# Keys and queries of a fused attention and expert layer: transposed in 32 rows a head, with the repeated rows written by transfers

## The chip, the cores and the metric

The kernel runs on one core of a Trainium2 chip. The metric is the device time of one execution in microseconds (us). The engines named here are TensorE (PE in the rows; its weight loads are PEld), VectorE (DVE), ScalarE (ACT), GpSimd (POOL) and SyncE, whose queue (SPq) issues every transfer of this kernel and does nothing else.

## The reference, cut to what matters

The input x is (4, 1024, 256): 4 batches, 1024 positions, 256 channels. Two layers follow each other, all in float32:

- A gated recurrence: x is normalised, two projections are made, and `state = tanh(p_t + state)` runs over the 1024 positions, one after the other, for all batches and channels at once. The gated states are normalised and added to x.
- A block on the rows of each 256-position piece: causal attention within the piece with 16 heads of 16 channels, then four experts.

```
h = _rms(x, n1_w)
q = _rms(heads(wq), qn_w);  k = _rms(heads(wk), kn_w);  v = heads(wv)
scores = einsum('bhqd,bhkd->bhqk', q, k) * HD ** (-0.5)        # causal
x = x + ao                                                      # softmax(scores) @ v, then @ wo.T
moe = wts[:, 0:1]*o0 + wts[:, 1:2]*o1 + wts[:, 2:3]*o2 + wts[:, 3:4]*o3
```

All 1024 positions of a batch attend causally to the positions before them. The four experts are chains of two to four products with gelu or silu between them, weighted by a top-2 gate.

## The kernel before, in words

**Units.** The time axis is cut into 4 chunks of 256 positions. A unit `u` (0 to 15) is 256 rows of 4 batches by 4 chunks: `c, b = divmod(u, 4)`. In chunk 0 a unit holds one row tile of 128 positions of each of two batches, in the other chunks two row tiles (`s` = 0, 1) of one batch. A unit can begin when the recurrence has passed its last position. It goes through these steps: gate and normalise (`pgate`, `ptr`, `pln`, `pu`), the projections (`qk`, `vm`), keys and queries (`kh`, `kt`, `kc`, `kst`; `qq`, `qt`, `qc`), the row maxima of the scores (`ktm`, `mxm`, `mxr`), their transposition into a bound (`mtr`, `mta`, `mtd`), the scores and their exponentials (`kts`, `sc`, `ex`, `msk`), the product with the values (`vl`, `av`), the output projection, and the experts (`up`, `gel`, `dn`, `da`), whose weights are loaded again for each unit (`wr`, 27 loads a unit into 6 buffers `WB`).

**Recurrence.** Each of the 1023 steps is an addition on GpSimd (`sadd`, line 1702) and a tanh on ScalarE (`stanh`, line 928). ScalarE does the kernel's other activations between them.

**Order.** `arrange()` (line 249) lists every step with its engine, an assumed duration, a due time and the steps it follows; `Plan.run()` (line 112) plays this through and writes down one fixed order for each engine. The due times are tables in the source (`START`, `AT`). On the chip each engine runs its list in that order and waits on semaphores, so a late step holds back all that stand behind it on its engine. The assumed durations decide the order alone.

**Keys and queries before.** Products are float32 in a reduced form, so each key and query is split into a high part (hi) and a low part (lo), and the score is `khi*qhi + khi*qlo + klo*qhi`. A head takes 64 columns of `QKP`: for keys hi, hi, lo, for queries hi, lo, hi (16 each), then a column of ones and 15 of zeros. VectorE writes them (lines 1490 and 1492). TensorE transposes two heads at a time, 8 transposes a row tile (`kt`, `qt`, line 1126), into two banks of the accumulator memory (`P2`). ScalarE copies 1024 columns out (lines 979 and 987): queries straight into `QT`, where they stay, keys into `KTs`, from which 4 transfers a row tile (`kst`, line 850) store them into `ktd` in memory. From there they are loaded twice for each unit, once for the maxima (`ktm`, lines 861 and 863) and once for the scores (`kts`, lines 883 and 885), as 128 rows: 64 of an even head, 64 of an odd one. The products read 64 rows. Row 48 of the keys is one, and row 48 of the queries is one until `mtd` (line 872) overwrites it with the negated maximum.

The lines the change touches: 249 to 430 (the plan), 545 to 550 (how much a transfer adds to its semaphore), 636 to 641 and 709 (buffers), 845 to 886 (transfers), 974 to 988 (ScalarE's copies), 1120 to 1182 (transposes and products), 1471 to 1492 and 1505 to 1510 (VectorE), 1663 to 1693 (constants on GpSimd).

Of the kernel before, what the change touches and what calls it, by code (L numbers as in the profile page):

```python
# [5 lines left out]
F32 = mybir.dt.float32  # L6
F32R = mybir.dt.float32r
# [12 lines left out]
KR = 64  # L20
# [24 lines left out]
           "Vs": 1, "QKP": 1, "KTs": 1, "QT": 2, "KT": 3, "VL": 2, "PT": 3, "AVS": 2, "AO": 1, "TV": 1,  # L45
# [4 lines left out]
DRAIN = 0.25  # L50
# [4 lines left out]
WINDOW, LOW, HIGH, FRESH = 3.413, 0.38, 0.75, 80.0  # L55

STALL = {"wsh": 0.3, "wsp": 0.45, "gll": 0.45, "kh": 0.12, "pgate": 0.15, "qq": 0.06, "hsc": 0.05, "fin": 0.05, "pln": 0.03, "pu": 0.03}
# [3 lines left out]
AT = {"piece": (-65.1, 79.3, 93.0, 117.5),  # L61
      "post": (73.5, 53.5, -11.6, 4.0),
      "prep": (-32.9, -50.6, -75.5, -31.9),
      "value": (-168.0, 5.7, -122.1, -102.7),
      "key": (-92.9, -70.4, 23.2, -60.9),
      "query": (-70.1, -15.7, -105.7, -9.8),
      "max": (-55.3, -48.9, -46.0, -51.3),
      "maxima": (1.8, 4.8, 14.5, 33.1),
      "bound": (97.6, -38.5, 63.2, 74.1),
      "score": (20.8, 39.5, 20.4, 48.1),  # L70
      "scores": (18.6, 9.7, 15.8, 8.7),
      "av": (18.9, -22.6, 2.7, 0.5),
      "merge": (36.4, -20.4, -11.9, 0.7),
      "out": (-203.1, 8.4, -74.1, -92.8),
      "gate": (-58.6, -112.8, -61.9, -36.5),
      "l1": (38.7, 246.6, 204.8, 191.9),
      "e0up": (141.5, 167.2, 99.3, 296.6),
      "l2": (241.4, 262.9, 274.5, 274.1),
      "e0dn": (304.8, 265.3, 456.7, -58.1),
      "e1": (248.8, 254.1, 341.0, 226.9),  # L80
      "l3": (253.5, 307.5, 179.0, 266.6),
      "e3dn": (182.7, 315.9, 233.6, 257.0),
      "e1dn": (285.7, 322.0, 304.5, 354.3),
      "l4": (216.1, 314.5, 172.6, 308.5),
      "e3up": (250.0, 261.2, 290.1, 275.3),
      "e3out": (240.7, 251.3, 293.6, 381.5),
      "fin": (203.7, 196.0, 239.1, 437.5)}


class Plan:  # L90
# [21 lines left out]
    def run(self):  # L112
# [15 lines left out]
        while True:  # L128
# [4 lines left out]
            for e in ready:  # L133
# [115 lines left out]
def arrange():  # L249
# [51 lines left out]
    add("pool", ("consts",), 6.6, 1.0, ("ident",))  # L301
# [16 lines left out]
    for u in range(NU):  # L318
# [33 lines left out]
        for s in range(2):  # L352
            add("dve", ("kh", u, s), 2.33, d, ("qrs", u), ("cqk", 0), ("consts",), take={"QKP": (("kt", u, s),)})
# [4 lines left out]
            add("pe", ("qt", u, s), 0.645, d0 + at["query"], ("qq", u, s), mode="128", take={"P2": (("qc", u, s),), **({} if s else {"QT": (("sc", u, 3, nkb - 1),)})}, lat=DRAIN)  # L358
            add("act", ("qc", u, s), act(1024), d0 + at["query"], ("qt", u, s), *([("qc", u, 0)] if s else []))
# [5 lines left out]
        for j, (g, planes) in enumerate(jobs):  # L365
            dj = d + at["maxima"] * j / len(jobs)
            add("sp", ("ktm", u, j), 0.35, dj - 5, *keys, *([("ktm", *prior["ktm"])] if "ktm" in prior else []), lat=4.5, take={"KT": (("mxm", u, ends[j]),)})
            prior["ktm"] = (u, j)
            for i, (j_, s, pl, k0, w) in enumerate(tiles):
# [6 lines left out]
                add("pe", ("mxm", u, i), 0.02 + w / 2400 + (0.065 if diag else 0.0), dj, ("ktm", u, j), ("qc", u, 0), ("qc", u, 1), ("consts",),  # L376
# [11 lines left out]
        for g in range(4):  # L388
# [3 lines left out]
            for h in range((nkb + 3) // 4):  # L392
                lastkb = min(4 * h + 3, nkb - 1)
                add("sp", ("kts", u, g, h), 0.35, dg - 5, *keys, *([("kts", *prior["kts"])] if "kts" in prior else []), lat=4.5, take={"KT": (("sc", u, g, lastkb),)})
# [115 lines left out]
class Signals:  # L510
# [34 lines left out]
    def step(self, key):  # L545
        if key not in self.plan.transfers:
            return 1
        if key[0] in ("gl", "ktm", "kts", "vl") and key[1] < B:
            return 32
        return {"vst": 64, "kst": 64, "mtd": 32}.get(key[0], 16)  # L550
# [34 lines left out]
def build(nc, A, out):  # L585
    ctx = ExitStack()
    with ctx:
# [48 lines left out]
        QKP = sb("QKP", [128, HEADS, KR], F32R)  # L636
        MT = sb("MT", [16, L], F32R)
        KTs = sb("KTs", [128, 8, 128], F32R)
# [70 lines left out]
        ktd = dram("ktd", (B, 4, 128, 2, T))  # L709
# [29 lines left out]
        def _(eng):  # L739
# [7 lines left out]
            for key in plan.order["sp"]:  # L747
# [97 lines left out]
                elif kind == "kst":  # L845
# [893 lines left out]
```

## Time and profile before

| | |
|---|---|
| median of 3 runs | 1584.79 us (1576.91 to 1586.72) |
| the profiled execution's own time | 1589.69 us |
| span of its profile | 1588.0 us |
| mean granted TensorE clock | 0.933 |
| TensorE busy | 1403.0 us, 88% |
| VectorE busy | 1098.6 us, 69% |
| ScalarE busy | 952.3 us, 60% |
| GpSimd busy | 319.2 us, 20% |
| transfers | 278.54 MB, their queue at 56.6% of the 16 transfer engines |

Busy time is the time in which an engine has an instruction under way. The granted clock is a share of TensorE's full clock, 2.4 GHz; at 0.5 it runs at 1.2 GHz. The transfer engines move the data; the queue on SyncE only issues. A stretch A:B is in us from the start of the span.

### The profile page before, as it was taken

How to read it: one execution, taken by the hardware profiler on the slowest of the kernel's cores; microseconds unless marked ns; L12 is line 12 of the kernel's file. 1: busy time of each engine (PE TensorE's matmuls, PEld its weight loads, DVE VectorE, ACT ScalarE, POOL GpSimd, SP SyncE). 2: the span in 40 equal slices, each digit the busy share in tenths (PEclk: the TensorE clock that was granted, in tenths of full speed). 3: DMA queues.
4: the chain of work that ended last, by engine and by line, in shares of the span. 5: the costliest groups of instructions: out<-in, count | busy, mean ns of one | idle time of the engine just before them, and what ended most of it. 6: DMA issues, size and time to landing. Idle time of an engine off the chain costs nothing. (4 is left out here: it accounts for less than half of the span.)

```text
span 1588.0 us, 33694 instructions
## 1 busy us (share of the span) xinstructions
PE 1403.0 (88%) x12320; PEld 1108.8 (70%) x12320; DVE 1098.6 (69%) x2916; ACT 952.3 (60%) x2092; POOL 319.2 (20%) x1146
## 2 busy tenths in 40 slices
PE   6915679999979799998998999999999999999997
PEld 3404567889867568688885577876686667857697
DVE  7776577553886975858888569786788777773342
ACT  2535465675556777775555673538546676468941
POOL 3343333223333323232332110001000010000000
PEclk9956578999998999899998899999999999999999
DMA  5585336754675545546656455665656657556343
GB/s 170 147 285 151 112 103 195 217 152 142 181 227 184 184 138 169 184 125 201 204 177 191 150 161 168 223 193 153 205 178 207 202 170 216 180 189 202 123 144 112
DMA packets 244276, 278.54 MB, mean 175 GB/s; under 512 B 37136, under 2 KB 167696, under 8 KB 243856
## 3 DMA queue, kind: packets, MB, share of 16 engines
q1 hardware_dynamic: 244112, 276.39, 56.6%
q8 instruction: 99, 1.62, 0.4%
q14 instruction: 65, 0.53, 0.1%
HBM read 234.18 MB, written 43.45 MB: 175 GB/s over the span
## 5 line engine op out<-in xcount | busy, mean ns | idle before, releaser
L1702 POOL TENSOR_TENSOR AD<-PX 128x8 f32<-128x8 f32 x1023 | 250.4, 245 | 553.3 <-ACT PX L928 537.3
L928 ACT ACTIVATE PX<-AD 128x8 f32<-128x8 f32 x1023 | 219.3, 214 | 232.0 <-POOL AD L1702 229.8
L996 ACT ACTIVATE work<-PS 128x1024 f32<-128x1024 f32 (+1 forms) x312 | 288.7, 960 | 79.5 <-PE PS L1042 77.8
L1501 DVE TENSOR_REDUCE mx<-PS 128x2 f32<-128x1024 f32 (+3 forms) x256 | 256.7, 1020 | 81.0 <-PE PS L1042 79.9
L1042 PE MATMUL PS<-work,vlx 128*32 128x256 f32 (+2 forms) x2816 | 240.6, 381 | 18.3 <-ACT work L996 7.5
L1042 PE MATMUL PS<-EP,u_e_l 128*128 128x256 f32 x1024 | 199.4, 289 | 6.9 <-DVE EP L1367 4.5
L1709 POOL TENSOR_SCALAR_AFFINE_SELECT work<-work 128x512 f32<-128x512 f32 x96 | 63.8, 674 | 638.1 <-ACT work L996 637.9
L1042 PE MATMUL PS<-WB,work 128*128 128x192 f32 x1024 | 181.2, 330 | 3.6 <-ACT work L1021 1.3
L1021 ACT ACTIVATE work<-PS 128x512 f32<-128x512 f32 x176 | 104.2, 596 | 132.7 <-PE PS L1042 131.2
L1042 PE MATMUL PS<-EP,WB 128*128 128x256 f32 x640 | 182.3, 285 | 0.0
L1042 PE MATMUL PS<-KT,QT 64*128 64x512 f32 (+3 forms) x768 | 151.9, 434 | 27.8 <-DVE mx L1501 12.9
L1042 PEld LDWEIGHTS PS<-EP,u_e_l 128*128 128x128 f32 x1024 | 164.0, 192 | 14.8 <-issue 10.3
L1042 PEld LDWEIGHTS PS<-WB,work 128*128 128x128 f32 x1024 | 164.9, 190 | 10.0 <-issue 4.0
L1042 PE MATMUL PS<-XF,WB 128*128 128x256 f32 x576 | 163.5, 284 | 0.0
L1042 PEld LDWEIGHTS PS<-work,vlx 128*32 128x32 f32 (+1 forms) x2816 | 87.6, 115 | 103.3 <-issue 49.6
L1042 PE MATMUL PS<-QT,KT 64*128 64x256 f32 (+1 forms) x1344 | 142.7, 315 | 15.9 <-ACT work L996 7.1
L1042 PEld LDWEIGHTS PS<-QT,KT 64*128 64x128 f32 x1344 | 99.9, 193 | 66.3 <-issue 45.6
L1042 PEld LDWEIGHTS PS<-KT,QT 64*128 64x128 f32 x768 | 72.8, 197 | 75.6 <-issue 27.1
L1042 PEld LDWEIGHTS PS<-EP,WB 128*128 128x128 f32 x640 | 124.3, 194 | 0.0
L1501 DVE TENSOR_REDUCE mxb<-PS 128x2 f32<-128x256 f32 (+3 forms) x128 | 104.7, 818 | 14.4 <-PE PS L1042 14.1
L1042 PEld LDWEIGHTS PS<-XF,WB 128*128 128x128 f32 x576 | 111.2, 193 | 0.1
L1021 ACT ACT_TABLE_LOAD x58 | 74.4, 1283 | 53.3 <-PE PS L1042 52.6
(170 smaller groups left out, 2345.8 us busy)
## 6 DMA issues: line engine op xcount, KB each, us to landing
KT<-ktd SPq DMA_DIRECT2D x112, 512.0 KB, 4.8
WB<-wlo_e_l SPq DMA_DIRECT2D x160, 256.0 KB, 3.0
WB<-wlo_e_up SPq DMA_DIRECT2D x64, 256.0 KB, 3.0
ktd<-KTs SPq DMA_DIRECT2D x128, 128.0 KB, 2.2
WB<-wlo_e_w SPq DMA_DIRECT2D x64, 256.0 KB, 2.9
WB<-wdn_e_down SPq DMA_DIRECT2D x64, 192.0 KB, 2.7
KT<-ktd SPq DMA_DIRECT2D x48, 256.0 KB, 3.5
KT<-ktd SPq DMA_DIRECT2D x32, 384.0 KB, 4.1
```

The source lines that it names most:

```text
L928: eng.activation(cur, AD[n % 2], ACT.Tanh).then_inc(of(*key), 1)
L996: eng.activation(pt[:, :, :, q0:L], two("sc", *a).rearrange("p a (l q) -> p a l q", l=2)[:, :, :, q0:L], ACT.Exp).then_inc(of(*key), 1)
L1021: eng.activation(half_of(hidden(u, name), h), one("up", u, name, h), ACT.Gelu).then_inc(of(*key), 1)
L1042: return eng.matmul(o, l, r, start=start, stop=stop, skip_group_check=skip)
L1501: eng.tensor_reduce(o, two("mxm", *a)[:, :, 0:w], AX, ALU.max, negate=True).then_inc(of(*key), 1)
L1702: eng.tensor_tensor(AD[n % 2], PX[c % 2][:, :, :, t], PX[(n - 1) // L % 2][:, :, :, (n - 1) % L], ALU.add).then_inc(of(*key), 1)
L1709: eng.affine_select(out=p, in_=p, compare_op=ALU.is_ge, fill=0.0, base=0, pattern=[[0, 2], [0, 2], [1, 128]], channel_multiplier=-1).then_ ...
```

## The change

Each head gets 32 columns instead of 64: hi and lo, once each. There are two `QKP` buffers instead of one. Four heads make one transpose, so a row tile takes 4 transposes for keys and 4 for queries, into one bank (`P1`), and ScalarE copies 512 columns. The repeated rows are made by transfers:

- `kst` stores keys with 8 transfers a row tile instead of 4. Each of four heads' row blocks is written as 32 rows (hi, lo) and again 16 rows (hi). `ktd` now has 48 rows a head instead of 64.
- `qst` is new: the queries are copied to a staging buffer `QTs`, and 8 transfers a row tile move them within the core's memory into `QT` (16 rows hi, then 32 rows hi, lo). The maxima now wait for `qst` of the second row tile, where they waited for ScalarE's copy.
- Every key load of `ktm` and `kts` becomes two, one for each parity of the head, of 48 rows each.
- The maxima read 48 rows, the scores 49. The row of ones is no longer loaded; GpSimd fills the three `KT` buffers with ones at the start, in place of filling `QKP`. The addition of 1 in `mta` becomes a copy.
- The plan's assumed durations, its due times and the constants of its clock model are changed, so that every engine's order can differ from before.

```diff
-KR = 64
+KR = 32
-           "Vs": 1, "QKP": 1, "KTs": 1, "QT": 2, "KT": 3, ...
+           "Vs": 1, "QKP": 2, "KTs": 1, "QTs": 1, "QT": 2, "KT": 3, ...
[...]
[...]
+STREAM = {"ptr": 0.6, "qtr": 0.6, "xtr": 0.6, "aot": 0.6, "mgt": 0.6, "mtr": 0.6, "kt": 0.65, "qt": 0.65, "gm": 0.05, "htr": 0.5}
-STAY = {"pe": 18.5, "act": 7.0}
+STAY = {"pe": 31.5, "act": 6.8}
-START = (114.6, 163.8, 192.7, 269.5, 332.7, 421.8, 507.9, 597.9, 743.8, 801.4, 926.0, 996.4, 1096.7, 1187.3, 1295.6, 1383.6)
+START = (111.5, 169.3, 217.5, 285.7, 325.4, 421.8, 511.2, 594.7, 746.0, 799.4, 931.6, 974.7, 1099.6, 1177.1, 1290.4, 1382.0)
...
-                        streamed[w] += t - t0
+                        streamed[w] += (t - t0) * STREAM.get(k[0], 0.95)
...
-    add("pool", ("consts",), 6.6, 1.0, ("ident",))
+    add("pool", ("consts",), 9.0, 1.0, ("ident",))
...
-            add("dve", ("kh", u, s), 2.33, d, ..., take={"QKP": (("kt", u, s),)})
-            add("pe", ("kt", u, s), 0.645, d, ("kh", u, s), mode="128", take={"P2": (("kc", u, s),), "KTs": (("kst", u, s),)}, lat=DRAIN)
-            add("act", ("kc", u, s), act(1024), d, ("kt", u, s))
-            add("sp", ("kst", u, s), 1.0, d, ("kc", u, s), lat=2.5)
-            add("dve", ("qq", u, s), 0.93, d0 + at["query"], ("kh", u, s), ("kt", u, s), take={"QKP": (("qt", u, s),)})
-            ...
+            add("dve", ("kh", u, s), 2.06, d, ..., take={"QKP": (("kt", u, s),)})
+            add("pe", ("kt", u, s), 0.33, d, ("kh", u, s), mode="128", take={"P1": (("kc", u, s),), "KTs": (("kst", u, s),)}, lat=DRAIN)
+            add("act", ("kc", u, s), act(512), d, ("kt", u, s))
+            add("sp", ("kst", u, s), 2.0, d, ("kc", u, s), lat=2.5)
+            add("dve", ("qq", u, s), 0.66, d0 + at["query"], ("kh", u, s), take={"QKP": (("qt", u, s),)})
+            ...
+            add("sp", ("qst", u, s), 2.0, d0 + at["query"], ("qc", u, s), *([("qst", u, 0)] if s else []), lat=2.5,
+                take=None if s else {"QT": (("sc", u, 3, nkb - 1),)})
...
-            add("sp", ("ktm", u, j), 0.35, ...
+            add("sp", ("ktm", u, j), 0.5 if c else 1.0, ...
...
-        ktd = dram("ktd", (B, 4, 128, 2, T))
+        ktd = dram("ktd", (B, 4, 2, 48, 2, T))
...                                                    # kst
-                    for g in range(4):
-                        eng.dma_start(ktd[b, g, :, :, 128 * t:128 * t + 128],
-                                      plain(KTs[:, 2 * g:2 * g + 2, :])).then_inc(of(*key), 16)
+                    for pl in range(2):
+                        for par in range(2):
+                            h = 32 * (2 * pl + par)
+                            dst = ktd[b, :, par, :, pl, 128 * t:128 * t + 128].rearrange("g r t -> r g t")
+                            eng.dma_start(dst[0:32], plain(KTs[h:h + 32])).then_inc(of(*key), 16)
+                            eng.dma_start(dst[32:48], plain(KTs[h:h + 16])).then_inc(of(*key), 16)
+                elif kind == "qst":
+                    ...
+                    for pl in range(2):
+                        for par in range(2):
+                            h, dst = 32 * (2 * pl + par), qt[64 * par:64 * par + 48, :, pl, 128 * s:128 * s + 128]
+                            eng.dma_start(plain(dst[0:16]), plain(QTs[h:h + 16])).then_inc(of(*key), 16)
+                            eng.dma_start(plain(dst[16:48]), plain(QTs[h:h + 32])).then_inc(of(*key), 16)
...                                                    # kts, chunks 1 to 3; ktm alike
+                    sp.wait_ge(*done("consts"))
-                        eng.dma_start(plain(keys_of(kt, 2, n)),
-                                      ktd[u % B, g, :, :, 512 * h:512 * h + n]).then_inc(of(*key), 16)
+                        for par in range(2):
+                            eng.dma_start(plain(keys_of(kt, 2, n)[64 * par:64 * par + 48]),
+                                          ktd[u % B, g, par, :, :, 512 * h:512 * h + n]).then_inc(of(*key), 16)
...                                                    # kt and qt on TensorE
-                    for p in range(8):
-                        ins = eng.transpose(ps[:, p // 4, 128 * (p % 4):128 * (p % 4) + 128].bitcast(F32R),
-                                            QKP[:, 2 * p:2 * p + 2, :].rearrange("p h r -> p (h r)"), identr)
+                    for g in range(4):
+                        x = QKP[place[src, "QKP"]][:, 4 * g:4 * g + 4, :].rearrange("p h r -> p (h r)")
+                        ins = eng.transpose(one(*key)[:, 128 * g:128 * g + 128].bitcast(F32R), x, identr)
...                                                    # mxm, and sc with + 49
-                    pe.wait_ge(*latest([("qc", u, 0), ("qc", u, 1)]))
+                    pe.wait_ge(*done("qst", u, 1))
-                        rows = slice(64 * par, 64 * par + 64)
+                        rows = slice(64 * par, 64 * par + 48)
...                                                    # kh and qq on VectorE
-                    step(eng.tensor_copy(pair, x.unsqueeze(2).to_broadcast([128, 16, 2, 16])))
+                    step(eng.tensor_copy(hi, x))
-                    eng.tensor_tensor(QKP[:, :, low:low + 16], x, QKP[:, :, 0:16].bitcast(F32), ALU.subtract).then_inc(of(*key), 1)
+                    eng.tensor_tensor(lo, x, plain(hi), ALU.subtract).then_inc(of(*key), 1)
...                                                    # consts on GpSimd
-                    step(eng.memset(QKP.bitcast(F32), 0.0))
+                    for kt in KT:
+                        step(eng.memset(plain(kt), 1.0))
-                    step(eng.memset(QKP[:, :, 48:49].bitcast(F32), 1.0))
```

## Rows read from the trace of the kernel before

**Rows 1.** The page, its first part: busy us (share of the span) and instructions.

```profile
PE 1403.0 (88%) x12320; PEld 1108.8 (70%) x12320; DVE 1098.6 (69%) x2916; ACT 952.3 (60%) x2092; POOL 319.2 (20%) x1146
```

**Rows 2.** Busy time by stretch: stretch, us, each engine (instructions), granted clock, transfer share, GB/s.

```profile
100.00:200.00 100.00, 52.42 (x426) 42.11 (x426) 65.84 (x194) 48.12 (x175) 36.19 (x146) 0.59 0.51 154
200.00:300.00 100.00, 88.08 (x752) 76.09 (x744) 69.57 (x233) 63.36 (x191) 30.65 (x124) 0.85 0.55 164
...
1300.00:1400.00 100.00, 98.54 (x902) 78.38 (x901) 76.81 (x148) 58.88 (x74) 2.56 (x4) 1.00 0.64 192
```

**Rows 3.** Chain of waits from 860 us to the end, shares by engine and line.

```profile
by line: PE PS L1042 69.4%; ACT work L996 5.9%; issue 3.7%; DVE mx L1501 2.7%; PE PS L1045 2.1%; PE PS L1126 1.9%; DVE mxb L1501 1.7%; DMA KT<-ktd 1.4%; ACT L996 1.0%; ACT work L1021 0.8%; POOL work L1709 0.7%; ACT L1021 0.6%; DMA out<-UU 0
```

**Rows 4.** TensorE's order of work at 402 us: start, us, instructions, [idle before, releaser].

```profile
402.88 0.66 PE L1045 MATMUL PS<-ident,G 128*128 128x128 f32 x4 [1.03 <-DVE G L1413]
```

**Rows 5.** Who waited for whom: us in total, times, longest.

```profile
PE PS L1042 <- ACT work L996: 15.3, 32, 1.2
PE PS L1042 <- DMA KT<-ktd: 12.8, 7, 4.7
```

**Rows 6.** TensorE's order of work from 908 to 916 us.

```profile
908.66 0.74 PE L1042 MATMUL PS<-QT,KT 64*128 64x256 f32 x8
...
911.49 0.81 PE L1126 MATMUL PS<-identr,QKP 128*128 128x128 f32 x8
912.23 0.51 PE L1042 MATMUL PS<-QT,KT 64*128 64x256 f32 x4
...
914.10 1.70 PE L1042 MATMUL PS<-wqkv,hT 128*128 128x256 f32 x12
```

**Rows 7.** Line 1126 by stretch: stretch, us, PE busy, PEld busy, clock, transfer share, GB/s.

```profile
860.00:1588.00 728.00, 19.95 (x184) 17.02 (x184) 0.98 0.57 176
```

**Rows 8.** Groups by line and shape: count, busy us, mean ns, idle before.

```profile
L987 ACT ACTIVATE QT<-PS 128x1024 fp32r<-128x1024 f32 x32 | 32.8, 1024 | 13.6 <-PE PS L1126 13.5
L979 ACT ACTIVATE KTs<-PS 128x1024 fp32r<-128x1024 f32 x32 | 32.7, 1022 | 9.1 <-PE PS L1126 8.3
...
L1490 DVE CAST QKP<-QKB 128x512 fp32r<-128x512 f32 x64 | 29.2, 456 | 18.0 <-PE PS L1126 16.9
...
L972 ACT ACTIVATE Vs<-PS 128x512 f32<-128x512 f32 x16 | 9.6, 598 | 5.1 <-PE PS L1042 5.0
```

**Rows 9.** The page's groups, the score matmuls.

```profile
L1042 PE MATMUL PS<-QT,KT 64*128 64x256 f32 (+1 forms) x1344 | 142.7, 315 | 15.9 <-ACT work L996 7.1
```

**Rows 10.** Transfer issues by line: duration ns min/median/max, first and last start.

```profile
L850 SPq DMA_DIRECT2D ktd<-KTs x128: 513/620/1396, 139.1 to 1338.8; - x128
L861 SPq DMA_DIRECT2D KT<-ktd x32: 519/612/614, 149.8 to 305.4; - x32
L863 SPq DMA_DIRECT2D KT<-ktd x80: 319/374/638, 448.9 to 1427.3; - x80
L883 SPq DMA_DIRECT2D KT<-ktd x32: 517/612/1467, 163.3 to 336.5; - x32
L885 SPq DMA_DIRECT2D KT<-ktd x80: 517/524/951, 465.8 to 1486.0; - x80
L872 SPq DMA_DIRECT2D QT<-MT x32: 667/694/972, 176.6 to 1448.0; - x32
```

**Rows 11.** Transfers by form: issues, KB each, median us from issue to landing.

```profile
ktd<-KTs SPq DMA_DIRECT2D x128, 128.0 KB, 2.2
```

**Rows 12.** The first unit's stores and loads in the queue's order of time.

```profile
139.12 9.10 SPq L850 DMA_DIRECT2D ktd<-KTs  x8
149.82 3.84 SPq L861 DMA_DIRECT2D KT<-ktd  x6
```

**Rows 13.** The first products of maxima on TensorE.

```profile
153.09 0.33 PE L1042 MATMUL PS<-KT,QT 64*128 64x128 f32 x2 [2.38 <-DMA KT<-ktd]
```

**Rows 14.** What the queue waited for, us in total, times, longest.

```profile
SPq L794 <- PE PS L1042: 523.5, 246, 8.7
```

**Rows 15.** GpSimd's fill of QKP: duration ns, start.

```profile
L1672 POOL MEMSET QKP<- x1: 957/957/957, 2.9 to 2.9; 128x1024 f32 x1
```

More of the change, by code:

```diff
@@ new lines @@
+AT = {"piece": (-65.9, 153.7, 123.4, 201.4),
+      "post": (72.6, 37.5, 49.8, -40.7),
+      "prep": (-70.5, -85.7, -81.5, -49.3),
+      "value": (-130.5, -16.5, -90.8, -207.4),
+      "key": (-101.3, -93.8, 12.1, -50.7),
+      "query": (-72.5, -22.3, -74.4, 27.9),
+      "max": (-59.5, -56.5, -90.7, -58.8),
+      "maxima": (4.2, 6.9, 6.2, 38.7),
+      "bound": (92.1, -24.2, -6.7, 63.2),
+      "score": (12.1, 37.8, -26.2, 42.4),
+      "scores": (16.3, 10.1, 13.1, 9.8),
+      "av": (22.3, -28.9, 12.1, 9.6),
+      "merge": (38.1, -28.6, 7.6, -20.1),
+      "out": (-276.1, -58.2, -98.8, -100.5),
+      "gate": (-72.2, -98.2, 13.3, 92.2),
+      "l1": (78.2, 227.7, 186.3, 197.3),
+      "e0up": (117.8, 172.1, 107.2, 286.2),
+      "l2": (237.2, 278.9, 224.7, 314.6),
+      "e0dn": (310.5, 380.5, 428.4, -102.3),
+      "e1": (255.0, 249.6, 316.5, 264.8),
+      "l3": (260.0, 266.6, 186.3, 277.0),
+      "e3dn": (156.2, 277.3, 288.1, 301.4),
+      "e1dn": (309.0, 333.5, 323.6, 417.3),
+      "l4": (195.7, 268.5, 188.1, 308.5),
+      "e3up": (204.1, 263.0, 289.7, 256.2),
+      "e3out": (135.5, 251.9, 390.0, 415.6),
+      "fin": (210.7, 237.6, 213.2, 516.9)}
@@ L366, in arrange @@
             dj = d + at["maxima"] * j / len(jobs)
-            add("sp", ("ktm", u, j), 0.35, dj - 5, *keys, *([("ktm", *prior["ktm"])] if "ktm" in prior else []), lat=4.5, take={"KT": (("mxm", u, ends[j]),)})
+            add("sp", ("ktm", u, j), 0.5 if c else 1.0, dj - 5, *keys, *([("ktm", *prior["ktm"])] if "ktm" in prior else []), lat=4.5, take={"KT": (("mxm", u, ends[j]),)})
             prior["ktm"] = (u, j)
@@ L375, in arrange @@
                 diag = k0 + w == 128 * rows[s][1] + 128
-                add("pe", ("mxm", u, i), 0.02 + w / 2400 + (0.065 if diag else 0.0), dj, ("ktm", u, j), ("qc", u, 0), ("qc", u, 1), ("consts",),
+                add("pe", ("mxm", u, i), 0.02 + w / 2400 + (0.065 if diag else 0.0), dj, ("ktm", u, j), ("qst", u, 0), ("qst", u, 1), ("consts",),
                     *([("mxm", u, i - 1)] if i else []), mode="64", take=take, lat=DRAIN)
@@ L393, in arrange @@
                 lastkb = min(4 * h + 3, nkb - 1)
-                add("sp", ("kts", u, g, h), 0.35, dg - 5, *keys, *([("kts", *prior["kts"])] if "kts" in prior else []), lat=4.5, take={"KT": (("sc", u, g, lastkb),)})
+                add("sp", ("kts", u, g, h), 0.5 if c else 1.0, dg - 5, *keys, *([("kts", *prior["kts"])] if "kts" in prior else []), lat=4.5, take={"KT": (("sc", u, g, lastkb),)})
                 prior["kts"] = (u, g, h)
@@ L547, in step @@
             return 1
-        if key[0] in ("gl", "ktm", "kts", "vl") and key[1] < B:
+        if key[0] in ("gl", "vl") and key[1] < B:
             return 32
-        return {"vst": 64, "kst": 64, "mtd": 32}.get(key[0], 16)
+        if key[0] in ("ktm", "kts"):
+            return 64 if key[1] < B else 32
+        return {"vst": 64, "kst": 128, "qst": 128, "mtd": 32}.get(key[0], 16)
     def sem(self, name):
@@ L635, in build @@
         hT = [sb(f"hT{i}", [128, 2, L], F32R) for i in range(2)]
-        QKP = sb("QKP", [128, HEADS, KR], F32R)
+        QKP = [sb(f"QKP{i}", [128, HEADS, KR], F32R) for i in range(BUFFERS["QKP"])]
         MT = sb("MT", [16, L], F32R)
-        KTs = sb("KTs", [128, 8, 128], F32R)
+        KTs = sb("KTs", [128, 4, 128], F32R)
+        QTs = sb("QTs", [128, 4, 128], F32R)
         Vs = sb("Vs", [128, 2, 16 * NV + 15])
@@ L867, in _ @@
                     c = u // B
-                    qt = QT[place[("qt", u, 0), "QT"]]
+                    qt = QT[place[("qst", u, 0), "QT"]]
                     sp.wait_ge(*done("mta", u))
@@ L1509, in _ @@
                     v.wait_ge(*done("mtr", u))
-                    eng.tensor_scalar(MT, one("mtr", u)[0:16, 0:256], 1.0, None, ALU.add).then_inc(of(*key), 1)
+                    eng.tensor_copy(MT, one("mtr", u)[0:16, 0:256]).then_inc(of(*key), 1)
                 elif kind == "avc":
```

84 lines of the change are left out of this document (33 added, 51 removed).

## The prediction, made before the changed kernel ran

> **What bounds the kernel now.** I read the engines' busy times first. TensorE is busy 88% of the span, the next engine 69% [rows 1]. The mean hides two regimes, so the table by stretch comes second. From 100 to 200 us TensorE is busy 52 of 100 us at a granted clock of 0.59: the first units wait on their own chain of small steps. From 200 us on it is busy 88 to 98 of 100 us, and from 1300 us at the full clock [rows 2]. Third is the chain of waits: from 860 us to the end 69.4% of it is line 1042, TensorE's products, and the transposes of line 1126 add 1.9%; ScalarE's and VectorE's lines of 0.6% and more are together 12.7% [rows 3]. Last, does the recurrence hold TensorE back? At 402 us, where unit 4 waits for its last position, TensorE stood idle 1.03 us [rows 4]. So past 200 us the kernel is a full TensorE queue: work taken from TensorE counts nearly whole, work taken from the others by their small share of the chain, and a delay in the first units counts unless later idle time takes it up.
>
> **TensorE.** A group of 8 transposes starts at 911.49 and the next work at 912.23: 0.74 us, 0.092 each [rows 6]. Four fewer save 0.37 us. There are 64 groups (16 units, 2 row tiles, keys and queries); 8 belong to units 0 and 1 and run before 200 us, where TensorE is idle half the time. 56 x 0.37 = 20.7 us. Bounds: the group of four in [rows 4] took 0.66 us against 0.81 for eight, which would leave 0.15 a group, 8 us; half of the mean busy time of a group (19.95 us over 184 / 8 = 23 groups, 0.87) gives 0.43, 24 us [rows 7]. I take 20.7, from the spacing, which is what a queue behind it feels. The products keep their columns and their count; no row shows a product of 48 or 49 rows, and I take it at the time of 64, with a rival below.
>
> **ScalarE, VectorE, banks.** ScalarE's copies of 1024 columns take 1.02 us, one of 512 columns 0.60 [rows 8]: 64 x 0.43 = 27 us less busy. ScalarE's lines are 8.3% of the chain [rows 3], which makes 2.3 us. VectorE's cast falls from 512 to 256 elements: 0.46 us each [rows 8], between nothing and half of it saved, I take 0.15 for its fixed part, 10 us of busy time and 0.5 us on the chain. Keys and queries now need one bank instead of two and hold it 0.4 us less, and the second `QKP` buffer ends the wait of VectorE's cast for the transposes, 16.9 us in all [rows 8], of which little is TensorE's. I put 2 us on both. Together 5 us; bounds 0 and 15.
>
> **The queue on SyncE.** Each row tile stores keys with 8 transfers instead of 4 (+128 in all) and moves queries with 8 (+256); key loads, 32 + 80 + 32 + 80 by lines 861 to 885, double (+224). That is 608 more issues, which no hidden engine pays for: they stand in the one queue that also issues the weight loads. The rows give an issue 0.32 us (the shortest of line 863) to 0.69 (line 872, also a move within the core's memory) [rows 10]. Size is not what sets it, since line 872 moves the least. I take 0.5. The total of 304 us is affordable: the queue spent 523 us on line 794 just waiting for weight buffers [rows 14]. What counts is what is late.
>
> - Unit 0. Its stores took from 139.12 to 148.2 and its first loads began at 149.82 [rows 12]; the first product of maxima waited 2.38 us for them [rows 13]. Now 8 more store issues and 16 query moves precede it, 24 x 0.5 = 12 us. About 3 us come back, from four copies that are 0.43 us shorter and transposes at the low clock. So 9 us late, in a stretch where TensorE has nothing else. Nothing covers this but the 12 us that TensorE idles from 200 to 300 [rows 2]. I take 5 us; bounds 0 and 25, the upper one if units 1 to 3 are late too.
> - Units 4 to 15. The first maxima wait for `qst`: 8 x 0.5 + 2.2 us to landing [rows 11] = 6.2 us, where the plan assumes 2.0 + 2.5 and a hop of 0.06. So it is 1.6 us later than the order was drawn for, and 12 units make 19 us. In the kernel before the plan took a key store at 1.0 us where four issues take 4 x 0.62 [rows 10], and TensorE still waited for key loads only 12.8 us in 7 waits [rows 5]. So most hides behind expert work: I take 5 us; bounds 0 and 28. Behind `qst` in the queue stand weight loads, held back 8 x 0.5 = 4 us; six buffers cover that if two bursts do not meet.
> - Key loads carry 96 rows instead of 128. Loads that are hidden gain nothing: 0.
>
> **The rest.** GpSimd fills three buffers instead of one, 2 x 0.96 us [rows 15], long before the first load at 149.82; behind it is the recurrence's first addition, which waits for the first projection. 0, at most 2. `mta` changes its operation and not its size: 0. The order is drawn anew. TensorE idles 185 us in all, 48 of them from 100 to 200 us, so under 10 us per 100 later, while the best stretch has 1.5 [rows 1, 2]. A new order can win or lose some of this; I take 0, and 15 us either way for the range.
>
> **Sum.** -20.7 - 5 + 5 + 5 = -16 us. Against the profiled execution's 1589.69 us that is 1574; the median of the runs is 4.9 us lower, so the forecast is 1568 to 1569. I say **1568 us**. A measurement of this kernel can tell about 1% (16 us) from no change.
>
> **Rivals.**
>
> - *The larger gain.* The delays hide wholly, and the upper bounds of the gains hold: -24 - 15 = -39 us, 1546. For it: TensorE hardly waited for transfers [rows 5]. Against: banks and ScalarE were small waits. 12%.
> - *It washes out.* In attention stretches TensorE is paced by ScalarE's exponentials and VectorE's maxima (5.9%, 2.7% and 1.7% of the chain [rows 3], 15.3 us of waits on ScalarE [rows 5]), so that half the saved 20.7 us turns into waits for them, and the two delays stay: 1585 - 10 - 5 + 10 = 1580, within 1% from 1570 to 1600. 20%.
> - *The queue becomes the bound* (slower). Place: the queue during chunk 0 and at each unit's first maxima. Price: 0.62 us for each store, 0.61 for each load, 0.69 for each query move [rows 10]. Unit 0 is late by 8 x 0.62 + 16 x 0.69 - 3 = 13 us. Each unit of chunk 0 needs 8 x 0.62 + 16 x 0.69 + 16 x 0.61 = 26 us more of the queue, some 5 us more than is free between its waits, 15 us for three units. Each later unit waits 8 x 0.69 + 2.2 - 4.56 = 3.1 us, less the 0.8 us that transposes and copies give back: 2.3 x 12 = 28. Together 56, less 26 of gains: +30 us, 1615. It decides from about 0.6 us an issue. For it: the plan assumes 0.25 us a transfer, less than any row; the first product already waited for a load. Against: the free time of the queue later on. 25%. The Trainium skill, "DMA: Bandwidth & Descriptors", section "Bandwidth", speaks for this case: it wants copies batched toward 1 MiB and calls those under 64 KB dominated by overhead, and this change splits them; that is a reason for this rival, not a term of it.
> - *The change does not do what it says.* Products of 48 or 49 rows may no longer share the array. Eight of 64 rows took 0.74 us, 0.093 each, twelve of 128 rows and the same 256 columns 1.70, 0.142 each [rows 6]. The difference on 1344 score products [rows 9] is 66 us: 1635 or more. 2%.
>
> **Chances.** The forecast, gain of 9 to 30 us, has 41%: 30% beyond 1%, 11% within. Faster by over 1%: 30 + 12 = 42%. Within 1%: 11 + 20 = 31%. Slower: 25 + 2 = 27%. The forecast's own range is 1555 to 1576. The range that should hold 8 in 10 takes in the larger gain and most of the slower case: 1544 to 1612.
>
> **What would show it.** Line 1126 at 256 transposes and half its busy time; line 979's and 987's copies at 0.6 us; the issues of the stores and moves at a median near 0.5 us (at 0.6 or more the queue rival gains); TensorE's waits for `QT` or `KT` transfers under 25 us past 200 us; the first product of maxima near 162 us (past 166: the queue rival); the score products at an unchanged mean. I am wrong if TensorE's busy time falls by 20 us and its idle time past 200 us grows by as much.

## The result and the profile after

The changed kernel takes 1700.26 us (median of 4 runs, 1698.21 to 1702.28), the kernel before 1584.6 beside it (4 runs): a ratio of 1.0736, 95% interval 1.0702 to 1.077. It is 116 us slower. The profiled execution has a span of 1699.9 us. These are the engines' busy times on its page:

```profile
PE 1413.7 (83%) x12064; PEld 1114.5 (66%) x12064; DVE 1092.2 (64%) x2916; ACT 908.1 (53%) x2078; POOL 314.8 (19%) x1147
```

The 256 transposes are gone and ScalarE does 44 us less, yet TensorE is busy 11 us longer than in [rows 1] and idle for 1699.9 - 1413.7 = 286 us instead of 185. The table by stretch (columns as in [rows 2]) shows where:

```profile
100.00:200.00 100.00, 33.25 (x218) 26.94 (x218) 54.03 (x158) 34.06 (x133) 26.49 (x110) 0.55 0.49 132
200.00:300.00 100.00, 73.47 (x592) 60.47 (x593) 55.82 (x198) 46.74 (x148) 22.52 (x96) 0.70 0.44 118
```

From 200 to 300 us TensorE ran 592 instructions in place of 752, at a granted clock of 0.70 in place of 0.85. In most stretches that grew idle the granted clock fell too, so more of the work ran at the lower of its two levels (1.2 GHz, not 2.4), and fewer instructions are busy for longer. Before 200 us the idle time grew by 19 us, after it from 103 to 185 us (busy time of the stretch 200 us to the end taken from its length, in both traces). The transfer engines are not what filled up: they move 265 MB instead of 279, and their share from 200 to 300 us is 0.44 in place of 0.55.

What TensorE waited for (us in total, times, longest), to be held against [rows 5]:

```profile
PE PS L1071 <- DMA QT<-QTs: 58.5, 6, 16.7
PE PS L1071 <- DMA KT<-ktd: 24.9, 13, 6.8
...
PE PS L1071 <- ACT work L1025: 20.5, 31, 3.9
```

The queue's issues by line (duration in ns min/median/max, first and last start), which answer [rows 10]:

```profile
L862 SPq DMA_DIRECT2D ktd<-KTs x128: 303/432/2184, 138.8 to 1378.5; - x128
L863 SPq DMA_DIRECT2D ktd<-KTs x128: 303/442/1646, 139.3 to 1378.9; - x128
L874 SPq DMA_DIRECT2D QT<-QTs x128: 592/602/1779, 142.6 to 1464.2; - x128
L875 SPq DMA_DIRECT2D QT<-QTs x128: 585/596/1362, 143.4 to 1464.8; - x128
L887 SPq DMA_DIRECT2D KT<-ktd x64: 543/596/1379, 153.2 to 358.9; - x64
L891 SPq DMA_DIRECT2D KT<-ktd x160: 302/423/2480, 511.4 to 1545.2; - x160
L913 SPq DMA_DIRECT2D KT<-ktd x64: 542/597/1471, 180.6 to 390.2; - x64
L917 SPq DMA_DIRECT2D KT<-ktd x160: 537/596/1636, 543.1 to 1599.8; - x160
```

Counts times medians over all lines that issue: 1121 issues and 506 us of the queue before (32% of the span), 1729 issues and 843 us after (50%); the single durations add up to 542 and 885 us. In the stretch from the first key store to the end of unit 0 it was 172 issues and 93 of 184 us before (51%), and is 326 issues and 175 of 236 us (74%). The issue time beside the transfer is not small here: a move of queries is issued in 0.60 us and lands in 2.1. The Trainium skill, "DMA: Bandwidth & Descriptors", section "Issuing engines are not separate DMA queues", says that the time to initiate a DMA is usually small relative to the DMA itself. By the rows above it is over a quarter of it, and it is serial in one queue while the transfers are not (moves start some 0.64 us apart and land 2.1 us after their start), so here the measurement decides.

**One late link, read from engine to engine.** The queue around unit 0 (start, us, engine, line, tile, count; single issues of a kind cut to the first and the last):

```profile
138.80 0.43 SPq L862 DMA_DIRECT2D ktd<-KTs  x1
...
142.63 0.71 SPq L874 DMA_DIRECT2D QT<-QTs  x1
...
153.21 5.04 SPq L887 DMA_DIRECT2D KT<-ktd  x8
158.30 2.17 SPq L852 DMA_DIRECT2D vd<-Vs  x4
160.52 0.62 SPq L874 DMA_DIRECT2D QT<-QTs  x1
...
165.03 0.59 SPq L875 DMA_DIRECT2D QT<-QTs  x1
```

The moves of row tile 1 stand behind eight key loads and four value stores. TensorE's first maxima need them; this is its order of work:

```profile
167.25 0.48 PE L1071 MATMUL PS<-KT,QT 48*128 48x128 f32 x2 [12.39 <-DMA QT<-QTs]
...
169.53 0.72 PE L1156 MATMUL PS<-identr,QKP 128*128 128x128 f32 x4 [0.47 <-DVE QKP L1522]
```

VectorE's next cast of keys or queries stands in its list behind the first reduction of those maxima:

```profile
167.90 0.83 DVE L1531 TENSOR_REDUCE mx<-PS 128x2 f32<-128x256 f32 x2 [11.72 <-PE PS L1071]
168.64 0.28 DVE L1520 CAST QKP<-QKB 128x256 fp32r<-128x256 f32 x1
```

So the next transposes are late, at 169.53, and their copy stands in ScalarE's list ahead of the recurrence's next step:

```profile
158.89 0.21 ACT L960 ACTIVATE PX<-AD 128x8 f32<-128x8 f32 x1 [0.31 <-POOL AD L1732]
170.35 0.60 ACT L1017 ACTIVATE QTs<-PS 128x512 fp32r<-128x512 f32 x1 [11.25 <-PE PS L1156]
170.84 0.21 ACT L960 ACTIVATE PX<-AD 128x8 f32<-128x8 f32 x1
```

And GpSimd, with the other half of each step:

```profile
171.13 0.21 POOL L1732 TENSOR_TENSOR AD<-PX 128x8 f32<-128x8 f32 x1 [11.75 <-ACT PX L960]
```

The recurrence, 1023 steps of some 0.54 us in a row where nothing halts it, stood still for 12 us because a queue that it never uses was late. A like halt, of 16 us, ends at 295 us: TensorE waits until 289 us, where twelve key loads precede eight moves (of SPq, then of PE):

```profile
274.84 7.60 SPq L887 DMA_DIRECT2D KT<-ktd  x12
282.48 0.60 SPq L874 DMA_DIRECT2D QT<-QTs  x1
```

```profile
289.22 0.58 PE L1071 MATMUL PS<-KT,QT 48*128 48x256 f32 x2 [13.55 <-DMA QT<-QTs]
```

There is a shorter path as well. `QTs` and `KTs` have one buffer each, so ScalarE's next copy waits until the transfers have read the last one. Of ScalarE's waits before the change none is on a transfer; after it these are:

```profile
ACT QTs L1017 <- DMA QT<-QTs: 18.1, 8, 4.4
...
ACT KTs L1011 <- DMA ktd<-KTs: 5.2, 4, 1.8
```

The sum of all such halts is in GpSimd's waits, first before, then after:

```profile
POOL AD L1702 <- ACT PX L928: 537.3, 989, 5.8
```

```profile
POOL AD L1732 <- ACT PX L960: 640.9, 990, 16.0
```

That is 104 us more. The last addition starts at 863.5 us before and at 961.2 after, 98 us later. A unit can't begin before the recurrence has passed its last position, and the end comes 112 us later. (The two don't go together so closely in every run; see the end of the part on why the prediction was wrong.) The addition that ends a unit puts it into milestones (ns min/median/max, first and last start), before and after:

```profile
L1645 DVE TENSOR_TENSOR UU<-UU,XR x16: 691/692/1156, 322.8 to 1584.6; 128x512 f32<-128x512 f32 x16
```

```profile
L1675 DVE TENSOR_TENSOR UU<-UU,XR x16: 691/692/695, 375.3 to 1696.5; 128x512 f32<-128x512 f32 x16
```

52 of the 112 us are lost by the end of unit 0.

### The profile page after: what moved, and what is told of

The parts are those of the page before. It is cut to its first block, busy times and chain, and to the rows that moved or that the text cites. A ratio compares the mean times of both kernels' runs of the same rounds, so it can differ in the third digit from the quotient of the medians.

```text
span 1699.9 us, 33820 instructions
## 1 busy us (share of the span) xinstructions
PE 1413.7 (83%) x12064; PEld 1114.5 (66%) x12064; DVE 1092.2 (64%) x2916; ACT 908.1 (53%) x2078; POOL 314.8 (19%) x1147
## 4 chain that ended last, share of the span: by engine, by line
PE 42%; SPq 6%; DMA 5%; DVE 5%; ACT 5%; issue 3%; POOL 0%; ACTq 0%; DVEq 0%; POOLq 0%
PE PS L1071 40%; ACT work L1025 3%; DMA KT<-ktd 2%; PE PS L1074 1%; DVE mx L1531 1%; SPq L874 1%; DMA WB<-wlo_e_l 1%; SPq L875 1%; SPq L862 1%; SPq L863 1%; ACT L1025 1%; SPq L917 1%; DMA WB<-wdn_e_down 1%; SPq L802 1%; DVE mxb L1531 0%
## 5 line engine op out<-in xcount | busy, mean ns | idle before, releaser
L1732 POOL TENSOR_TENSOR AD<-PX 128x8 f32<-128x8 f32 x1023 | 246.5, 241 | 655.4 <-ACT PX L960 640.9
L1071 PE MATMUL PS<-KT,QT 48*128 48x512 f32 (+3 forms) x768 | 151.6, 437 | 84.0 <-DMA QT<-QTs 58.5
L1071 PE MATMUL PS<-EP,u_e_l 128*128 128x256 f32 x1024 | 203.1, 292 | 14.9 <-DVE EP L1397 5.9
L1071 PE MATMUL PS<-WB,work 128*128 128x192 f32 x1024 | 193.8, 346 | 11.0 <-DMA WB<-wdn_e_down 7.5
L1071 PEld LDWEIGHTS PS<-WB,work 128*128 128x128 f32 x1024 | 177.9, 202 | 16.6 <-DMA WB<-wdn_e_down 7.2
L1071 PEld LDWEIGHTS PS<-EP,u_e_l 128*128 128x128 f32 x1024 | 167.8, 196 | 21.7 <-issue 16.5
L1071 PE MATMUL PS<-QT,KT 49*128 49x256 f32 (+1 forms) x1344 | 146.9, 323 | 40.3 <-DMA KT<-ktd 14.5
L1071 PEld LDWEIGHTS PS<-QT,KT 49*128 49x128 f32 x1344 | 102.9, 200 | 98.0 <-issue 57.1
L1071 PEld LDWEIGHTS PS<-KT,QT 48*128 48x128 f32 x768 | 74.0, 202 | 126.1 <-issue 89.7
L1661 DVE SCALAR_TENSOR_TENSOR UU<-PS,wts,UU 128x192 f32<-128x192 f32 x128 | 47.3, 411 | 107.7 <-PE PS L1071 107.6
```

What stands on the lines that cost most here:

```text
L1071: return eng.matmul(o, l, r, start=start, stop=stop, skip_group_check=skip)
L1661: ins = eng.scalar_tensor_tensor(U, ps[:, t, 0:NO], wts[:, u % 4, t, e_:e_ + 1], U, ALU.mult, ALU.add)
L1732: eng.tensor_tensor(AD[n % 2], PX[c % 2][:, :, :, t], PX[(n - 1) // L % 2][:, :, :, (n - 1) % L], ALU.add).then_inc(of(*key), 1)
```

## The experiments

Theory Q: the 608 more issues hold up the queue, and through the in-order lists everything else. Rivals over the runs: the size of the key loads, the products of 48 and 49 rows, the new due times, the place of the moves in the queue. All times are medians; "issues" counts the transfers of the whole kernel; the three marks are the first product of maxima, the end of unit 0 and the recurrence's last addition, in us, from each profile. The kernel before took 1582 to 1590 us beside these runs and each ratio is against that time, so a difference between two times of the table is good to some 8 us, and the marks are of one execution each.

```
kernel          issues  us      ratio [95%]               maxima  unit 0  last step
before          1121    1584.6  1                         153.1   322.8   863.5
e9_loads224     1345    1620.95 1.0202 [1.0144, 1.026]    155.1   330.7   884.6
e1_half         1473    1629.73 1.0255 [1.0204, 1.0306]   160.8   344.8   895.1
e7_split352     1473    1675.02 1.0532 [1.0475, 1.0588]   159.1   348.6   917.6
e6_moves4       1601    1668.02 1.0486 [1.0443, 1.0528]   162.7   358.4   929.2
e11_redraw      1729    1662.82 1.0509 [1.0477, 1.0541]   166.8   363.3   899.3
after           1729    1700.26 1.0736 [1.0702, 1.077]    167.3   375.3   961.2
e10_movefirst   1729    1723.91 1.0853 [1.0791, 1.0915]   161.0   373.2   963.6
e8_oldtab       1729    1777.27 1.1182 [1.1122, 1.1243]   167.0   387.8   965.7
e4_split608     1729    1784.39 1.1211 [1.1163, 1.1259]   166.1   379.4   988.2
```

**Half the stores and moves.** Four stores and four moves of 48 rows a row tile, in the order of the changed kernel, with the same bytes. Some rows now hold other data than they should: what is left out is the right content of keys and queries.

```diff
-   eng.dma_start(dst[0:32], plain(KTs[h:h + 32])).then_inc(of(*key), 16)
-   eng.dma_start(dst[32:48], plain(KTs[h:h + 16])).then_inc(of(*key), 16)
+   h = min(h, 80)
+   eng.dma_start(dst, plain(KTs[h:h + 48])).then_inc(of(*key), 16)
...                                                    # the moves alike
```

> The changed kernel with 4 stores and 4 query moves a row tile in place of 8 and 8: each copies 48 rows that lie side by side, so the repeated rows hold other data than they should; the bytes, every engine's order and all waits stay. Theory Q (the issues in the one transfer queue are the cost): 256 of the 608 added issues go, 128 stores of about 0.44 us and 128 moves of 0.60 us, 133 us of queue time; the time falls by a third to a half of the 115 us added, to 1640 to 1660, and TensorE's wait for the query moves (58.5 us) halves. Theory P (the new order is bad by itself, whatever the queue does): 1690 to 1700.

Measured 1629.73 us, 70 us less than the change for 256 issues less, which is more than Theory Q had said. Theory P, by which the order is at fault and nothing comes back, fell. ScalarE's waits for the moves fell from 18.1 to 1.8 us, and TensorE's for the moves fell to:

```profile
PE PS L1071 <- DMA QT<-QTs: 34.1, 4, 10.5
```

**Only half the moves** (the same edit on the moves alone).

> The changed kernel with 4 query moves of 48 rows a row tile in place of 8 (repeated rows hold other data), stores and loads as changed, order unchanged. 128 issues of 0.60 us go. e1 took 256 issues of stores and moves away and won 70 us. Theory Q2: the moves are the later link and wait behind the stores, so they hold 40 to 60 of the 70: 1640 to 1660. If stores count as much: 1665.

1668.02 us: 32 us for 128 issues. The stores' half is then worth about 38 us, though a store takes 0.43 us to issue and a move 0.60. Both kinds count at about the same rate, 0.25 and 0.30 us an issue.

**The key loads merged again.** `ktd` gets its 128 rows back, each load is one transfer, and the rows of ones are filled in by 16 transfers at the start.

```diff
-   for par in range(2):
-       eng.dma_start(plain(keys_of(kt, 2, n)[64 * par:64 * par + 48]),
-                     ktd[u % B, g, par, :, :, 512 * h:512 * h + n]).then_inc(of(*key), 16)
+   eng.dma_start(plain(keys_of(kt, 2, n)), ktd[u % B, g, :, :, 512 * h:512 * h + n]).then_inc(of(*key), 16)
...                                                    # ktm alike; the fill
```

> The changed kernel with each key load as one transfer of 128 rows again (keys kept in 64 rows a head in memory, rows 48 to 63 filled with ones once, early); order and waits unchanged otherwise. Theory Q: 224 issues of 0.42 to 0.60 us go, about 115 us of queue time; 1650 to 1675. If the smaller bytes of the 48-row loads were worth something, the gain is less. Theory P: 1690 to 1705.

> Both of the two edits before together: 480 of the 608 added issues go, the order stays that of the changed kernel. Theory Q: 1595 to 1625, since 128 query moves and their latency before the first maxima are left. Theory P: 1680 or more, and then it is the order that costs.

1735.48 us (ratio 1.0913 [1.0858, 1.0968]) and 1652.9 (1.0393 [1.0345, 1.0441]), both slower than their partners. The cause is my fill, in the queue's order of time:

```profile
21.70 37.06 SPq L820 DMA_DIRECT2D ktd<-KT  x16
```

It held the queue for 37 us in the middle of the first loads, and the first maxima came at 201.2 and 196.7 us. So the run does not answer its question, and was made again with the 16 transfers spread between others:

> As e2 (one load of 128 rows in place of two of 48), but the fill of rows 48 to 63 is issued one transfer at a time between others, so that it does not hold the queue for 37 us at the start as it did in e2. 1735 - 36 = 1699 is what e2 leaves for the loads: no gain. Theory Q1 (every issue costs alike): 1640 to 1670, by 224 issues. Theory Q2 (only issues that stand between a finished copy and the first maxima cost, that is stores and moves; loads are asked for ahead): 1690 to 1705.

1719.17 us (1.0809 [1.0756, 1.0861]), the first maxima at 185.5: the fill still costs, and the time lies above the ranges of both theories. What can be read is the time from the first maxima to the end of the span: 1532.6 us in the change, 1530.7 here; 1462.2 with half the stores and moves, 1458.7 with merged loads as well. By this measure merging 224 loads of 48 rows gives 2 to 4 us in the changed kernel, no more than executions of one kernel differ by. That the larger transfers (a third more bytes) take back what the issues save is argued and not shown.

**The issues without the change.** The kernel before, its orders kept, with 608 more issues: loads and stores in two halves of 64 rows, and eight stores of 16 rows to an unused array behind each key store.

```diff
-   eng.dma_start(ktd[b, g, :, :, 128 * t:128 * t + 128], plain(KTs[:, 2 * g:2 * g + 2, :])).then_inc(of(*key), 16)
+   for p in (0, 64):
+       eng.dma_start(ktd[b, g, p:p + 64, :, 128 * t:128 * t + 128],
+                     plain(KTs[p:p + 64, 2 * g:2 * g + 2, :])).then_inc(of(*key), 16)
+ for i in range(8):
+     eng.dma_start(spare[s, i], plain(KTs[16 * i:16 * i + 16, 0:4, :])).then_inc(of(*key), 16)
...                                                    # the loads in two halves
```

> The kernel before, its order, its transposes and its copies untouched, with 608 more issues in the queue: every key load and key store cut into two halves of 64 rows (352 issues), and 8 small stores of 16 rows to an unused array behind each key store (256). No query waits on them. Theory Q: most of the loss appears without any other part of the change, 1640 to 1680. Theory P: the queue has room (it waited over 500 us for weight buffers), so 1585 to 1605.

1784.39 us: 195 to 200 us more, far above the 1640 to 1680 of Theory Q, with every transpose, copy and product as before. The waits show the same halts on the other transfer (TensorE, then ScalarE and GpSimd):

```profile
PE PS L1052 <- DMA KT<-ktd: 78.0, 20, 12.8
...
ACT KTs L989 <- DMA spare<-KTs: 63.8, 13, 11.4
...
POOL AD L1712 <- ACT PX L938: 668.5, 989, 13.1
```

The second row shows that this run adds more than issue time. The small stores read `KTs` and count for its semaphore, so ScalarE's next key copy waits for them, 63.8 us in all, and so do the key loads. Neither the kernel before nor the change has a wait of that size (none, and 18.1 + 5.2 us). So the 195 us are the price of 608 more transfers with the waits that hang on them, not of their issue time alone.

**Split in steps**: without the eight small stores (352 more), and with the loads alone (224 more).

> The kernel before, order untouched, with key loads and key stores cut into halves of 64 rows (224 + 128 more issues), without the 256 small stores of e4. e4 was 195 us slower. Theory Q1: 352 of 608 issues, 110 us, 1700. Theory Q2: loads are nearly free and 128 stores cost about 0.25 us each: 1620 to 1640.

> The kernel before, its order untouched, with every key load cut into two of 64 rows (224 more issues, the same bytes), stores whole. e7 had these and 128 more store issues, and was 85 us slower. If each issue counts alike: 224/352 of it, 54 us, 1640. If loads are asked for ahead and only the stores cost: 1590 to 1600. If the loads cost here but gave nothing when merged in e5, then fewer bytes of 48 rows paid their second issue back in the changed kernel.

1675.02 and 1620.95 us. Both lie between the cases that were set out. Step by step an added issue costs 31/224 = 0.14 us for loads, 54/128 = 0.42 for the store halves and 109/256 = 0.43 for the small stores, the last two with ScalarE's waits for the stores in them (14.9 and 63.8 us). The steps were taken in this order only, each on top of the one before. A reason why loads are the cheapest is that they can be issued ahead of need, while a store or move is waited for at once; no run separates that from their place in the order. e7_split352 and e1_half have the same 1473 issues, and e1_half, with the change's shorter copies and its new tables, is 45 us faster. That does not show what the savings are worth, since the next run puts 77 us on the tables.

**The tables of before in the changed kernel**: `START`, `AT`, `STAY` and the clock constants put back.

> The changed kernel with the due times and clock constants of the kernel before (the durations of the changed steps stay as changed), so the orders differ from both. Theory Q (the queue costs, whatever the order): 1690 to 1760. If the new tables were the fault: 1600 to 1650.

1777.27 us, above what Theory Q had said, so the new due times are no fault of the change: they win 70 to 77 us of it. With the old tables ScalarE also loads its activation tables 140 times instead of 102, at 1.28 us each, and TensorE's clock is 0.863. The run has the tables and the number of issues of e4_split608, and the two times (ratios 1.1182 and 1.1211) can't be told apart. But e4_split608 has waits that the change has not, so what the change saves by itself stays unmeasured.

**The moves pulled ahead** of loads and value stores that directly precede them (11 of 32 groups).

```diff
...                                                    # order: the queue's list
+ for key in [k for k in order if k[0] == "qst"]:
+     i = j = order.index(key)
+     while order[j - 1][0] in ("ktm", "vst", "xl", "gl"):
+         j -= 1
+     order.insert(j, order.pop(i))
...
```

> The changed kernel with nothing but this: in the queue's list the query moves of a row tile are pulled ahead of key loads, value stores and unit loads that stood directly before them (11 of 32 groups of moves; in unit 0 the moves of row tile 1 go ahead of 8 key loads and 4 value stores). Issues, bytes and all other orders stay. Theory R (a late move stops TensorE, behind it a copy of ScalarE, behind that the recurrence): unit 0's first maxima start about 7 us earlier than 167 us, the recurrence's last step ends 10 to 25 us earlier, the time is 1665 to 1690. Theory Q (only the sum of issue time counts): 1700 unchanged.

My theory that the place of the moves was the fault fell. The first maxima came 6 us earlier (161.0), and the run took 1723.91 us, 19 to 24 more than the change, where Theory Q had said unchanged. The waits moved from one transfer to the other:

```profile
PE PS L1077 <- DMA KT<-ktd: 63.9, 18, 10.5
...
PE PS L1077 <- DMA QT<-QTs: 14.6, 2, 12.8
```

What goes ahead of the loads makes the loads late; 78.5 us of waits here, 83.4 in the change.

**Redrawn with the measured issue times.** The planner is told what a transfer takes of the queue, and the due times are searched again.

```diff
- add("sp", ("kst", u, s), 2.0, d, ("kc", u, s), lat=2.5)
+ add("sp", ("kst", u, s), 3.5, d, ("kc", u, s), lat=2.0)
- add("sp", ("qst", u, s), 2.0, d0 + at["query"], ("qc", u, s), ..., lat=2.5,
+ add("sp", ("qst", u, s), 4.8, d0 + at["query"], ("qc", u, s), ..., lat=2.1,
...                                                    # loads, value stores, bound's moves; START, AT, STAY
```

> The changed kernel, every instruction as it is, in another order. The planner's constants for SP's queue are set to what the traces show: a key store 3.5 us of issue and 2.0 us to land (plan of the change: 2.0 and 2.5), the moves of a row tile 4.8 us and 2.1 us (2.0 and 2.5), the key loads of the maxima 2.4, 1.2, 0.85, 0.85 us by chunk (1.0, then 0.5), of the scores 2.4 us in chunk 0 and 1.2 us later (1.0 and 0.5), a value store 1.9 us (0.8), the bound's moves 1.4 us (0.6); then due times, start times and the two stay constants are searched anew under these costs. Theory Q (the added issues hold up the queue, each list waits in its own order for the next, and a good part of the loss is that the orders were drawn for a queue that is cheaper than it is): stretch 139 us to the end of unit 0 shorter than 230 us (236 in the changed kernel, 184 before), time 1620 to 1665 us. Rival C (the loss is the capacity of the queue, which no order gives back: chunk 0 needs its 175 us of issues in any order, and the order drawn for the change is as good as another): 1690 to 1715 us, with waits moved from one line to another, as when the moves were pulled ahead. Rival O (due times fitted to a plan don't carry over to the chip, as with the tables of before in the changed kernel): above 1720 us.

1662.82 us: 37 us less than the change, with the same instructions (by the nearest ends of the two intervals, 1.0541 and 1.0702, at least 25 us). Stretch 139 us to the end of unit 0: 228 us, 236 in the change, 184 before. TensorE's waits and GpSimd's:

```profile
PE PS L1071 <- DMA QT<-QTs: 36.1, 5, 13.8
...
PE PS L1071 <- DMA KT<-ktd: 6.5, 3, 5.0
```

```profile
POOL AD L1732 <- ACT PX L960: 577.9, 993, 8.9
```

This fits Theory Q, and rival C in part. How much of the 37 us the measured issue times gave is not shown: the search drew all due times anew, and no search under the old issue times was run beside it. By the end of unit 0, 40 of the 52 us stay lost in the new order, where the queue's issues fill 78% of the stretch (counts times medians, as above); after it the loss falls from 59 us to 30 (last unit's end against before, less that of unit 0: 111.9 - 52.5 and 70.6 - 40.5). No order tried makes the change faster than the kernel before, which remains the fastest version seen. Whether a longer search would is open.

## Why the prediction was wrong

I forecast 1568 us and a range of 1544 to 1612; it took 1700.

**TensorE's term** was about right. A group of four transposes after the recurrence, and what follows it:

```profile
968.88 0.53 PE L1156 MATMUL PS<-identr,QKP 128*128 128x128 f32 x4
969.33 0.74 PE L1071 MATMUL PS<-QT,KT 49*128 49x256 f32 x8
```

0.45 us from start to start against 0.74 [rows 6]: 0.29 a group, where I took 0.37, so 16 us for 20.7. But the term was counted as time of the kernel, and it counts only where TensorE is the bound; before the change that was 86 to 99 of 100 us past 200 us and not 88 to 98, as I read it. Nor had the sum a term for the clock: TensorE is busy 11 us longer with 16 us less of transposes, so by my estimate some 27 us of its time come from the lower clock. The copies and VectorE's cast came out as said, at 0.60 us for 1.02 and 0.29 for 0.46 [rows 8]:

```profile
L1017 ACT ACTIVATE QTs<-PS x32: 578/597/609, 140.0 to 1459.5; 128x512 fp32r<-128x512 f32 x32
...
L1520 DVE CAST QKP<-QKB x64: 271/294/689, 135.6 to 1394.1; 128x256 fp32r<-128x256 f32 x64
```

ScalarE's busy time fell by 44 us where I said 27. The copies are 27 of them; 18 are 14 fewer loads of its activation tables (102 for 116, 1.28 us each), which the new order brought and I had not foreseen.

**The price of an issue** was right as well: 0.5 us assumed, 0.42 to 0.60 measured, 337 us in all where I said 304. Landing in 2.1 us matches the 2.2 taken.

**The step that failed** is "The total of 304 us is affordable: the queue spent 523 us on line 794 just waiting for weight buffers". That wait [rows 14] is an average over a run in which the queue was already busy for half of the stretch of unit 0, and it sits between issues that cannot be exchanged: the queue waits there for a buffer, with whatever comes next in the list behind it. It was still 408 us after the change:

```profile
SPq L802 <- PE PS L1071: 407.9, 219, 8.4
```

So slack and loss stand side by side in the same queue. I should have made the sum for 139 to 323 us alone: 154 more issues, some 82 us, had to fit into 184 us of which 93 were taken. Instead I priced unit 0's delay at 5 us and that of units 4 to 15 at 5 us, and let both end where they arose. Measured, 52 us were lost by the end of unit 0 and 59 after it.

**Unit 0 late by 9, cost 5.** The first product came at 167.3 us for 153.1, 14 us late, against "near 162"; my own text called past 166 the sign of the queue rival. With the moves pulled ahead (e10_movefirst) it came at 161.0, so some 6 of the 14 us are eight key loads and four value stores that stand before the moves of row tile 1 and that my 24 x 0.5 left out. What was not in the sum at all is the propagation: TensorE's list stands, ScalarE's copy behind it stands, and the recurrence behind that. I had dismissed the recurrence on one wait of 1.03 us at 402 us [rows 4], which said that it was not late before the change, not that it had room. 12 us of halt at 159 us are 12 us for all that follows a position, and unit 0's end was 52 us late. That each of its transfers met the same full queue is my reading of the 74%; no run takes the 52 us apart. The single buffer of `QTs`, for which ScalarE waited 18.1 us, was not in the sum either.

**Units 4 to 15, cost 5.** TensorE's waits for `QT` and `KT` past 200 us are 29.4 + 24.3 = 54 us, where I wanted under 25 and before had 4.3. That bound, which I named as a test, fell. My sign of being wrong had two halves. TensorE's idle time past 200 us grew by 82 us, four times what it named; its busy time, which was to fall by 20 us, rose by 11.

**The rivals.** The queue rival had the mechanism, the place and the prices (its 0.62, 0.61 and 0.69 were at or above what was measured), but its 56 us of cost are 116 in truth, and 132 if TensorE's 16 us counted in full, because it added local delays and let each one end where it arose. The products of 48 and 49 rows cost what those of 64 did:

```profile
L1071 PE MATMUL PS<-QT,KT 49*128 49x256 f32 (+1 forms) x1344 | 146.9, 323 | 40.3 <-DMA KT<-ktd 14.5
```

323 ns for 315 [rows 9], with the clock lower, against the 50% more that this rival's 0.142 for 0.093 us means; the rival is dead. "Washes out" failed in both its parts: the waits on ScalarE rose only from 15.3 to 20.5 us.

Left open: how the 59 us after unit 0 divide between queue waits, the lower clock (0.894 granted for 0.933) and the recurrence. The recurrence is one path and not the whole price. In e8_oldtab it ends only 4 us later than in the change (965.7 and 961.2), and the run takes 77 us longer, with TensorE busy for 1473 us instead of 1414; in e11_redraw it ends 62 us earlier, and the run takes 37 us less. Open, too, is whether the moves would do better in another engine's queue: no run shows it.

## What to carry to other kernels

Where one queue issues for all, cost an added transfer by its issue time in the densest stretch and not by the queue's idle time over the run; here 0.14 us each for loads and 0.42 for halves of stores came through to the end, in the order in which they were added. Follow a late transfer through every in-order list to the slowest serial chain, even if the chain never touches a transfer, and look for single buffers that a transfer has to free. Give a planner the issue times of the trace: the order searched with them was 37 us faster, though how much of it they account for was not separated.

## What the runs showed of the hardware

An issue's time follows neither bytes nor rows. A store of 16 rows takes what one of 32 rows takes (0.44 and 0.43 us), and key loads of 48 rows take 0.60 us where those of 128 rows took 0.61 in chunk 0 [rows 10]; later it is 0.42 for 0.37 and 0.60 for 0.52. Two loads for one thus take about twice the issue time or more. So do halves of 64 rows in the kernel before: 0.61 us a store in e7_split352, where the whole took 0.62, and 0.60 us a load in e9_loads224. The change's two stores of 32 and 16 rows take 1.4 times the one of 128 rows (0.87 us for 0.62). A move within the core's memory took 0.60 us for either 16 or 32 rows. The fill of e2_wide, whose source is one tile read four times over, took 2.57 us a transfer at the median:

```profile
L820 SPq DMA_DIRECT2D ktd<-KT x16: 426/2572/2577, 21.7 to 56.2; - x16
```
